# A three-stage decoder layer: a smaller move in memory, the last batch's router earlier, its last norm and store tile by tile

## The chip, the core and the metric

The kernel runs on one core of one Trainium2 chip. The metric is the device time of one execution in microseconds; lower is better. TensorE does the matrix products, VectorE (DVE), ScalarE (ACT) and GpSimd (POOL) the elementwise work, and SyncE (SP) issues all DMAs. Each engine works through its own instruction stream in order, and the engines wait for each other only at semaphores.

## The reference, cut to what matters

For 16 batches of 256 tokens with 512 channels, three sublayers follow each other, each added to its input and then normalised over the channels:

```
x = layernorm(x + attention(x) @ Wo + bo)      # 16 heads of 128, 4 KV heads, rotary, causal softmax
x = layernorm(x + wkv(w, u, k=x, v=context))   # running maximum and decayed sums over the tokens
x = layernorm(x + ffn(x))
# ffn(x):
h      = silu(x @ rw1.T + rb1)                 # 64 hidden channels
logits = h @ rw2.T + rb2 + gates               # 16 experts
coeff  = softmax over the top 2 of logits, zero elsewhere
out    = x @ W.T + bias + sum_e coeff[e] * (x @ A[e].T) @ B[e].T     # rank 16 each
```

## The kernel before

Every fp32 operand of a large product is split into a high and a low part, and a product is three matmuls (lines 527 to 529): high by high, high by low, low by high. TensorE does all of them in one stream.

The attention runs over 256 head positions (32 pairs of a half of the heads and a batch, 8 heads each). `run` walks through slots n; in each slot an engine does, for different heads at fixed lags, projection, scores, transposed probabilities, value product and output product. The weights come in as 40 raw pieces (`load_piece`), which ScalarE copies to the high part and DVE subtracts to the low part (`splits`, the subtraction is L1405). `SPLIT_AT` says in which slot ScalarE splits a piece; DVE does it one slot later (`behind=1`), at the end of its slot; SP issues the load up to three slots earlier. Ten staging areas in the WKV buffers hold raw pieces; the piece of head 4's query weights is the ninth and sits in the buffer `ED`.

In slot 3 DVE multiplies the third query head by the cosines (L1162, on ScalarE's bias at L772), then makes the low part of a V tile (L1192). TensorE's projections use two PSUM banks in turn, and so the projection of the fourth head waits for that V tile's low part (`proj_free`). The rotated half of a head pair is fetched by two DMAs, SW<-QB (L422, L423), POOL multiplies it by the sines (L1008), adds it (L1011) and makes the low part Ql (L1019), on which the scores (L596) wait.

The WKV recurrence of a batch ("tail") and the feed-forward stage ("step") are laid into the same slots at lags given by tables. A step k has three parts, and different batches stand at different stages in it: batch k-1 is turned, k-2 goes through router and low-rank products, k-3 through the dense product, k-4 through the last norm. Batches are counted in order of their feed-forward; the last is 15. So in step 17 TensorE does, in this order: low-rank products and router input of batch 15 (part 0), turn of batch 14's weighted low-rank rows (L700); dense(0) of batch 14, turn of batch 15's hidden tile (L712), in part 1; dense(1) of batch 14, logits of batch 15 (L721, four matmuls, on `hid_copied` from ScalarE), second low-rank product of batch 14, in part 2. In step 18 TensorE turns batch 15's weighted rows first (L700, on `weighted` from POOL), then does its dense products.

Between logits and `weighted` lie DVE's top 2 (L1382 to L1397) and POOL's coefficients (L1109 to L1113) and weighting (L1118). Behind the dense and low-rank products DVE adds the residual, a 128-token tile at a time (L1350, `out_sum`), the first tile in part 2 of step k and the second in part 0 of the next; then `norm_stats` (L1236, L1239, L1241) takes both tiles, POOL makes the inverse root and the shift (L1087 to L1091), ScalarE scales both tiles (L942), and SP stores the batch with one DMA of 512 KB (L485).

Buffers are allocated in order of their `sb` calls: W (81920 bytes per partition) first, then smalls, tables, Bo, XR, X and the rest.

Of the kernel before, what the change touches and what calls it, by code (L numbers as in the profile page):

```python
# [18 lines left out]
EPS = 1e-5  # L19
# [10 lines left out]
for i in range(PAIRS):  # L30
    f = i % 2
# [9 lines left out]
def ro_buf(b):  # L41
# [23 lines left out]
NP = JL + 2 + 2 * HEADS  # L65

FIRST_ORDER = [PK, PK + 1, PQ, PQ + 1, PV, PV + 1] + list(range(PQ + 2, NP))
SPLIT_AT = [[-6, -6, -2, -2, -6, -6, 0, 1, 1, 2, 3, 4] + [h // 2 + 4 for h in range(HEADS)],
            [7, 8, 10, 11] + [h + 11 for h in range(HEADS)] + [h + 19 for h in range(HEADS)]]
RELOAD_AT = [-10, -9, -6, -5] + [h - 6 for h in range(HEADS)] + [h + 3 for h in range(HEADS)]  # L70
KEEP_AT = [2, 3, 4, 5] + [h + 4 for h in range(HEADS)] + [h + 9 for h in range(HEADS)]
# [7 lines left out]
TAIL_BATCH = [b for i in range(PAIRS) for b in (2 * i + 1, 2 * i)]  # L79
# [95 lines left out]
def decoder(nc, xt, xn, ctxt, wraw, small, bo, wf, wl, wb, fbias, trig_t, late_t, out):  # L175
    fp32, fr, u32 = mybir.dt.float32, mybir.dt.float32r, mybir.dt.uint32
    ALU, ACT = mybir.AluOpType, mybir.ActivationFunctionType

    ctx = ExitStack()
    with ctx:  # L180
        def sb(name, shape, dt=fp32):
            return ctx.enter_context(nc.sbuf_tensor(name, shape, dt))
# [12 lines left out]
        wq_tile = lambda i, h, kc: W[:, PQ + h, i, kc * HD:(kc + 1) * HD]  # L195
        wo_tile = lambda i, h: W[:, PO + h, i, :]

        smalls = sb("smalls", [P, 160])
        cols = lambda at, n: smalls[:, at:at + n]
        by_half = lambda a: a.rearrange("p (f h) -> p f h", f=HALVES)  # L200
        Bk, Bq, Bv = by_half(cols(0, 4)), by_half(cols(4, 16)), by_half(cols(20, 4))
        Wb, Ub = cols(24, KC), cols(28, KC)
        Iota, Rb2, Gates, Rb1, Rw2 = cols(32, 16), cols(48, 16), cols(64, 16), cols(80, HID), smalls[0:HID, 144:160]

        late = sb("tables", [P, TT * C + P])
        tables = late[:, 0:TT * C]
        Cos, Sin, Mask = tables[:, 0:T], tables[:, T:2 * T], tables[:, TT * C - P - T:TT * C]
        Ident = late[:, TT * C:TT * C + P]
        Bo = sb("Bo", [P, C])

        XR = sb("XR", [P, KC, T])
# [75 lines left out]
        HST = SW[0:HID, 0, :]  # L287
        HB, HE = (SW[:, 1, a * P:(a + 1) * P].rearrange("p (a k) -> p a k", a=TT) for a in range(2))
        LOW = sb("LOW", [P, TT, EXP * RANK])
        Fb = Bo  # L290
        per_row = lambda a, n: a.rearrange("p (a k) -> p a k", a=1).to_broadcast([P, TT, n])
        STF = sb("STF", [P, 2, TT, 6])
        MVF = sb("MVF", [P, 2, TT, 2])
        VEF = sb("VEF", [P, 2, TT])
        RSF = sb("RSF", [P, 2, TT])
        NMF = sb("NMF", [P, 2, TT])

        s_flat = S[:, :, :].rearrange("p a n -> p (a n)")
# [92 lines left out]
        def run(eng, slot, splits=None, ffn_weights=None, step=None, ahead=0, behind=0):  # L391
# [11 lines left out]
            for n in range(FIRST_STEP_BEHIND, STEPS):  # L403
                for part in range(3):
                    step(n, part)

        def stage_of(n, lag):
            return n - lag if 0 <= n - lag < BATCH else None

# [3 lines left out]
        def _(sp):  # L413
# [55 lines left out]
            def step(n, part):  # L469
                f = stage_of(n, 0)  # L470
                if f is not None and part == 0:
                    b = TAIL_BATCH[f]
                    if f >= 2:
                        sp.wait_ge(biased, f - 1)
                        sp.wait_ge(f_turned, TT * (f - 1))
                    elif f == 1:
                        sp.wait_ge(q_lo, ALL // 2)
                    else:
                        sp.wait_ge(x2_out[2], x2_stored(13))
                    sp.wait_ge(x2_out[ro_buf(b)], x2_stored(b))  # L480
                    sp.dma_start(XF[f % 2], mixed[b, :, :].rearrange("(a p) c -> p a c", p=P)).then_inc(f_in[f % 2], 16)
                f = stage_of(n, 4)
                if f is not None and part == 2:
                    sp.wait_ge(f_done, f + 1)
                    sp.dma_start(out[TAIL_BATCH[f], :, :].rearrange("(a p) c -> p a c", p=P), OUT[f % 2]).then_inc(f_out[f % 2], 16)  # L485

            def load_piece(u):
                if u >= STAGES:
# [30 lines left out]
            sp.dma_start(late[:, TT * C - P - T:TT * C + P], late_t).then_inc(const_in, 16)  # L519
            run(sp, slot, splits, ffn_weights, step, ahead=AHEAD)  # L520
            for i in range(2):
                sp.wait_ge(f_out[i], 16 * BATCH // 2)

        @block.tensor
        def _(pe):
# [128 lines left out]
            def step(n, part):  # L654
                def turn_x2(t):
                    f = stage_of(n, 1)
                    if f is not None:
# [8 lines left out]
                            last = nc.tensor.transpose(bank[t][:, c * P:(c + 1) * P], XF[f % 2][:, t, c * P:(c + 1) * P], Ident[:, :])  # L666
                        last.then_inc(f_turned, 1)

                def dense(t):
                    f = stage_of(n, 3)  # L670
                    if f is not None:
                        if f == 0 and t == 0:
                            pe.wait_ge(acc_read, READS[POS - 1] + 1)
                            pe.wait_ge(w_lo, HALVES * NP + 2 * KC)
                        above(pe, f_sum, TT * (f - 1) + t + 1)
                        for k in range(KC):
                            last = three(bank[5 + t][:, :], [x[:, f % 2, k, t * P:(t + 1) * P] for x in X],
                                         [wf_tile(i, k) for i in range(2)], k == 0, False)
                        last.then_inc(dense_done, 1)
# [22 lines left out]
                elif part == 1:  # L702
                    dense(0)
                    turn_x2(0)
                    f = stage_of(n, 2)
                    if f is not None:
                        pe.wait_ge(silu_done, f + 1)
                        if f == 0:
                            pe.wait_ge(ot_lo, ALL // 2)
                        above(pe, lg_b, f)  # L710
                        for t in range(TT):
                            last = nc.tensor.transpose(bank[4][0:HID, t * P:(t + 1) * P], HE[:, t, :], Ident[:, :])  # L712
                        last.then_inc(hid_turned, 1)
                else:
                    dense(1)
                    turn_x2(1)
                    f = stage_of(n, 2)
                    if f is not None:
                        pe.wait_ge(hid_copied, f + 1)
                        for a in range(TT):  # L720
                            last = nc.tensor.matmul(bank[4][:, T + a * EXP:T + (a + 1) * EXP], HST[:, a * P:(a + 1) * P], Rw2, start=True, stop=True)  # L721
                        last.then_inc(logits_done, 1)
                    f = stage_of(n, 3)
                    if f is not None:
                        pe.wait_ge(wt_lo, f + 1)
# [11 lines left out]
        def _(act):  # L737
# [161 lines left out]
            def step(n, part):  # L899
# [26 lines left out]
                elif part == 1:  # L926
# [10 lines left out]
                        copy(HST, bank[4][0:HID, 0:T]).then_inc(hid_copied, 1)  # L937
                    f = stage_of(n, 4)
                    if f is not None:
                        act.wait_ge(f_shift, f + 1)  # L940
                        for t in range(TT):
                            last = nc.scalar.activation(OUT[f % 2][:, t, :], OUT[f % 2][:, t, :], ACT.Identity,  # L942
                                                        bias=NMF[:, f % 2, t:t + 1], scale=RSF[:, f % 2, t:t + 1])
                        last.then_inc(f_done, 1)
                else:
                    x_hi_tile(1)
                    f = stage_of(n, 2)
# [27 lines left out]
        def _(pool):  # L975
# [106 lines left out]
            def step(n, part):  # L1082
                f = stage_of(n, 4)
                if f is not None and part == 0:
                    pool.wait_ge(f_ve, f + 1)
                    above(pool, f_done, f - 1)
                    gp.tensor_tensor(RSF[:, f % 2, :], VEF[:, f % 2, :], Mhalf[:, :], ALU.pow).then_inc(f_rs, 1)  # L1087
                    pool.wait_ge(f_rs, f + 1)
                    gp.tensor_tensor(NMF[:, f % 2, :], MVF[:, f % 2, :, 0], RSF[:, f % 2, :], ALU.mult).then_inc(f_rs2, 1)
                    pool.wait_ge(f_rs2, f + 1)  # L1090
                    gp.tensor_scalar(NMF[:, f % 2, :], NMF[:, f % 2, :], -1.0, None, ALU.mult).then_inc(f_shift, 1)  # L1091
                f = stage_of(n, 2)
                if f is not None and part == 1:
                    pool.wait_ge(f_in[f % 2], 16 * (f // 2 + 1))
# [31 lines left out]
        def _(dve):  # L1126
# [104 lines left out]
                probabilities(n)  # L1231
                tail(n, 0)

            def norm_stats(tiles, par, stats, mv, ve, done):
                for t in range(TT):
                    v.bn_stats(stats[:, par, t, :], tiles[:, t, :])  # L1236
                dve.drain()
                for t in range(TT):
                    v.bn_aggr(mv[:, par, t, :], stats[:, par, t, :])  # L1239
                dve.drain()  # L1240
                v.tensor_scalar(ve[:, par, :], mv[:, par, :, 1], EPS, None, ALU.add).then_inc(done, 1)  # L1241

            def norm_shift(par, mv, rs, nm):
                v.scalar_tensor_tensor(out=nm[:, par, :], in0=mv[:, par, :, 0], scalar=-1.0, in1=rs[:, par, :],
# [90 lines left out]
            def step(n, part):  # L1335
# [16 lines left out]
                if part == 0:  # L1352
                    out_sum(4, 1)
                    f = stage_of(n, 4)
                    if f is not None:
                        dve.wait_ge(f_sum, TT * f + TT)
                        above(dve, f_shift, f - 1)
                        norm_stats(OUT[f % 2], f % 2, STF, MVF, VEF, f_ve)
                    f = stage_of(n, 2)
                    if f is not None:  # L1360
                        dve.wait_ge(hid_read, TT * f + TT)
# [13 lines left out]
                else:  # L1375
                    x_lo_tile(1)
                    f = stage_of(n, 2)
                    if f is not None:
# [19 lines left out]
                        dve.wait_ge(top_p2, f + 1)  # L1398
                        dve.wait_ge(lg_sum, f + 1)
                    out_sum(3, 0)  # L1400

            def splits(hf, i):
                u = nth_piece(hf, i)
# [72 lines left out]
```

## Time and profile before

| | |
|---|---|
| median of 3 runs | 1619.72 us (1618.47 to 1620.61) |
| the profiled execution | 1619.31 us |
| its span, first to last instruction | 1617.5 us |
| TensorE matmuls busy | 1554.8 us, 96% |
| DVE, ACT, POOL busy | 83%, 69%, 63% |
| granted TensorE clock, mean | 0.989 of full |

Busy shares are means over the whole span. TensorE is full nearly everywhere but at the two ends, so the views that count are the timelines and the chain of waits there. All positions are microseconds from the span's start.

### The profile page before, as it was taken

The numbers are of one execution on the slowest core, as the hardware profiler recorded it, in microseconds if no ns is written. First come the engines' busy times: TensorE is split into PE (matmuls) and PEld (weight loads), VectorE is DVE, ScalarE is ACT, GpSimd is POOL, SyncE is SP. The second block draws the span as 40 slices with busy tenths as digits, with TensorE's granted clock in tenths as the row PEclk, the third lists the DMA queues.
The fourth block names the chain that finished last, engine by engine and source line by source line (L and its number), as shares of the span: only waits on it lengthen the run. The fifth ranks groups of instructions, "written<-read, shape, count | busy, mean of one in ns | idle before, by whom it ended". The sixth has DMA issues, their size and how long they took to land.

```text
span 1617.5 us, 32631 instructions
## 1 busy us (share of the span) xinstructions
PE 1554.8 (96%) x10464; PEld 1411.9 (87%) x10464; DVE 1341.2 (83%) x3431; ACT 1117.2 (69%) x2995; POOL 1013.3 (63%) x852
## 2 busy tenths in 40 slices
PE   7999999999999999999999999999999977989997
PEld 7899999999999999999999999999999866777885
DVE  6776698889888988898989898888988885867864
ACT  6877787877787778777877787878777764334332
POOL 3665586758675767576767676767676642735653
PEclk9999999999999999999999999999999998999999
DMA  8766344324442444244424442444244412121211
GB/s 291 249 215 217 112 141 147 112 73 152 143 131 65 146 149 136 55 149 147 137 59 151 151 137 60 151 151 137 60 147 153 142 51 86 53 87 70 79 66 52
DMA packets 81624, 202.61 MB, mean 125 GB/s; under 512 B 10416, under 2 KB 11056, under 8 KB 81456
## 3 DMA queue, kind: packets, MB, share of 16 engines
q1 hardware_dynamic: 81456, 200.53, 39.4%
q8 instruction: 85, 1.39, 0.3%
q14 instruction: 83, 0.68, 0.1%
HBM read 120.80 MB, written 37.75 MB: 98 GB/s over the span
## 4 chain that ended last, share of the span: by engine, by line
PE 80%; DVE 8%; issue 3%; POOL 3%; ACT 2%; DMA 1%; DVEq 1%; SPq 0%; ACTq 0%; POOLq 0%
PE bank L527 24%; PE bank L528 23%; PE bank L529 23%; PE bank L651 5%; PE bank L596 2%; PE bank L642 1%; PE bank L634 1%; PE bank L597 1%; DMA SW<-QB 1%; DVE PS L1302 1%; DVE QS L1295 1%; PE bank L666 1%; DVE ED L1313 1%; DVEq L1383 1%; DVE RC L1162 0%
## 5 line engine op out<-in xcount | busy, mean ns | idle before, releaser
L527 PE MATMUL bank<-Xh,W 128*128 128x256 f32 x1280 | 363.6, 284 | 10.8 <-DVE W L1405 7.2
L528 PE MATMUL bank<-Xl,W 128*128 128x256 f32 x1280 | 362.1, 283 | 0.0
L529 PE MATMUL bank<-Xh,W 128*128 128x256 f32 x1280 | 361.8, 283 | 0.0
L1019 POOL TENSOR_TENSOR Ql<-RC,Qh 128x512 fp32r<-128x512 f32 x128 | 170.1, 1329 | 213.0 <-ACT Qh L739 213.0
L754 ACT ACTIVATE S<-S,NM 128x128 f32<-128x128 f32 (+1 forms) x512 | 228.1, 447 | 66.4 <-DVE NM L1147 65.9
L527 PEld LDWEIGHTS bank<-Xh,W 128*128 128x128 f32 x1280 | 242.9, 190 | 13.6 <-DVE Xl L1208 7.2
L739 ACT ACTIVATE PTh<-bank 128x384 fp32r<-128x384 f32 x256 | 125.1, 489 | 173.6 <-PE bank L651 173.6
L1008 POOL TENSOR_TENSOR SW<-SW,tables 128x512 f32<-128x512 f32 x128 | 170.2, 1330 | 116.8 <-DMA SW<-QB 116.7
L528 PEld LDWEIGHTS bank<-Xl,W 128*128 128x128 f32 x1280 | 243.4, 190 | 0.0
L529 PEld LDWEIGHTS bank<-Xh,W 128*128 128x128 f32 x1280 | 243.3, 190 | 0.0
L739 ACT ACTIVATE S<-S,RL 128x128 f32<-128x128 f32 (+1 forms) x512 | 203.5, 447 | 31.5 <-DVE RL L1154 31.4
L527 PE MATMUL bank<-W,OTh 128*128 128x512 f32 x512 | 203.6, 398 | 10.8 <-DVE OTl L1217 7.1
L528 PE MATMUL bank<-W,OTh 128*128 128x512 f32 x512 | 203.8, 398 | 0.0
L529 PE MATMUL bank<-W,OTl 128*128 128x512 f32 x512 | 203.2, 397 | 0.0
L1011 POOL TENSOR_TENSOR RC<-RC,SW 128x512 f32<-128x512 f32 x128 | 180.4, 1409 | 18.9 <-POOL SW L1008 0.9
L527 PE MATMUL bank<-W,Xh 128*128 128x256 f32 (+2 forms) x512 | 167.1, 326 | 1.7 <-DVE RC L1162 1.4
L528 PE MATMUL bank<-W,Xh 128*128 128x256 f32 (+2 forms) x512 | 163.4, 319 | 0.0
L529 PE MATMUL bank<-W,Xl 128*128 128x256 f32 (+2 forms) x512 | 163.3, 319 | 0.0
L1162 DVE SCALAR_TENSOR_TENSOR RC<-bank,smalls,tables 128x256 f32<-128x256 f32 x256 | 119.5, 467 | 42.5 <-ACT QB L772 42.4
L1133 DVE TENSOR_TENSOR PTl<-bank,PTh 128x384 fp32r<-128x384 f32 x256 | 141.1, 551 | 2.9 <-ACT PTh L739 2.3
L1143 DVE TENSOR_TENSOR S<-bank,tables 128x128 f32<-128x128 f32 x256 | 72.5, 283 | 78.0 <-PE bank L529 77.6
L651 PE MATMUL bank<-tables,S 128*128 128x128 f32 x768 | 126.2, 273 | 1.0 <-DVE PTl L1133 1.0
(155 smaller groups left out, 4446.6 us busy)
## 6 DMA issues: line engine op xcount, KB each, us to landing
W<-kept SPq DMA_DIRECT2D x140, 512.0 KB, 4.4
SW<-QB SPq DMA_DIRECT2D x256, 128.0 KB, 2.3
kept<-W SPq DMA_DIRECT2D x40, 512.0 KB, 4.7
XR<-XR SPq DMA_DIRECT2D x64, 128.0 KB, 2.3
RO<-in_xn SPq DMA_DIRECT2D x16, 512.0 KB, 4.0
KVT<-in_ctxt SPq DMA_DIRECT2D x16, 512.0 KB, 4.3
mixed<-RO SPq DMA_DIRECT2D x16, 512.0 KB, 4.0
XR<-in_xt SPq DMA_DIRECT2D x15, 512.0 KB, 5.1
```

Of the source, the lines that this page charges most:

```text
L527: nc.tensor.matmul(dst, lhs[0], rhs[0], start=first, stop=False)
L528: nc.tensor.matmul(dst, lhs[0], rhs[1], start=False, stop=False)
L529: return nc.tensor.matmul(dst, lhs[1], rhs[0], start=False, stop=last)
L651: last = nc.tensor.transpose(pt_ps[:, k * P:(k + 1) * P], S[:, g % 2, k * P:(k + 1) * P], Ident[:, :])
L739: return nc.scalar.activation(dst, src, ACT.Copy, **kw)
L754: last = nc.scalar.activation(S[:, i, c], S[:, i, c], ACT.Exp, bias=NM[:, i, t:t + 1], scale=-1.0, accum_out=L[:, i, t:t + 1])
L1008: gp.tensor_tensor(SW[:, :, :], SW[:, :, :], both(Sin), ALU.mult).then_inc(q_sin, 1)
L1011: gp.tensor_tensor(RC[:, i % 2, :, :], RC[:, i % 2, :, :], SW[:, :, :], ALU.add).then_inc(q_summed, 1)
L1019: gp.tensor_tensor(Q[1][:, :, :], RC[:, i % 2, :, :], Q[0][:, :, :], ALU.subtract).then_inc(q_lo, 1)
L1133: v.tensor_tensor(PT[1][:, g % 4, :], pt_ps[:, 0:P + T], PT[0][:, g % 4, :], ALU.subtract).then_inc(pt_lo, 1)
L1143: v.tensor_tensor(S[:, i, 0:P], s_ps[:, P:T], Mask[:, 0:P], ALU.add).then_inc(masked, 1)
L1162: v.scalar_tensor_tensor(out=RC[:, g // 2 % 2, g % 2, :], in0=proj_ps("Q", g, 0), scalar=Bq[:, SEQ[g // HEADS][0], h:h + 1], in1=Cos[:, :] ...
```

## The change

There are four edits. The small table `smalls` (640 bytes per partition) is allocated behind `LOW`, and the four statistics buffers of the last norm (96, 32, 16 and 16 bytes) ahead of `Bo`. The split of head 4's query weights goes from slot 1 to slot 2. In step 17 the logits of batch 15 come right behind its L712 in part 1, instead of behind dense(1). And for batch 15 alone, the last norm and the store go tile by tile: DVE takes tile 0's statistics behind its sum in part 2 of step 18, POOL and ScalarE do a tile at a time, and SP issues two stores of 256 KB.

```
-SPLIT_AT = [[-6, -6, -2, -2, -6, -6, 0, 1, 1, 2, 3, 4] + [h // 2 + 4 for h in range(HEADS)],
+SPLIT_AT = [[-6, -6, -2, -2, -6, -6, 0, 1, 2, 2, 3, 4] + [h // 2 + 4 for h in range(HEADS)],
...
-        smalls = sb("smalls", [P, 160])          # now behind LOW
...
+        STF = sb("STF", [P, 2, TT, 6])           # were behind LOW; MVF, VEF, RSF too
...
@@ SP, part 2 of a step, stage 4
+                        for t in range(TT):
+                            sp.wait_ge(f_done, f + t + 1)
+                            sp.dma_start(rows[:, t, :], OUT[f % 2][:, t, :]).then_inc(f_out[f % 2], 16)
...
@@ TensorE, part 1 of a step, behind the turn of the hidden tile
                         last.then_inc(hid_turned, 1)
+                        if f == LAST:
+                            logits()
                 else:
                     dense(1)
                     turn_x2(1)
-                    f = stage_of(n, 2)
-                    if f is not None:
-                        pe.wait_ge(hid_copied, f + 1)
-                        for a in range(TT):
-                            last = nc.tensor.matmul(bank[4][:, T + a * EXP:T + (a + 1) * EXP], HST[:, a * P:(a + 1) * P], Rw2, start=True, stop=True)
-                        last.then_inc(logits_done, 1)
+                    if stage_of(n, 2) != LAST:
+                        logits()
...
@@ ScalarE
-                        act.wait_ge(f_shift, f + 1)
                         for t in range(TT):
+                            act.wait_ge(f_shift, f + 1 + t * (f == LAST))
...
-                        last.then_inc(f_done, 1)
+                            if f == LAST or t == TT - 1:
+                                last.then_inc(f_done, 1)
...
@@ GpSimd
+                    for k, those in enumerate((slice(0, 1), slice(1, 2)) if f == LAST else (slice(0, TT),)):
+                        pool.wait_ge(f_ve, f + k + 1)
...
@@ DVE, norm_stats over a range of tiles; part 0, then part 2
-                        norm_stats(OUT[f % 2], f % 2, STF, MVF, VEF, f_ve)
+                        norm_stats(OUT[f % 2], f % 2, STF, MVF, VEF, f_ve, range(f == LAST, TT))
...
                     out_sum(3, 0)
+                    if stage_of(n, 3) == LAST:
+                        dve.wait_ge(f_sum, TT * LAST + 1)
+                        dve.wait_ge(f_shift, LAST - 1)
+                        norm_stats(OUT[LAST % 2], LAST % 2, STF, MVF, VEF, f_ve, range(1))
```

## Rows read from the trace of the kernel before

**Rows 1.** Windows, mid-kernel: busy of PE, PEld, DVE, ACT, POOL, clock, DMA share, GB/s
```profile
200.00:400.00 200.00, 199.65 (x1408) 183.80 (x1407) 179.35 (x453) 154.85 (x423) 140.20 (x101) 1.00 0.40 123
```

**Rows 2.** Chain of waits around the last logits: start us, us, what
```profile
1587.57 0.44 PE bank L700 x4
...
1590.81 0.22 PE bank L712 x2
...
1593.80 0.56 PE bank L721 x4
...
1598.46 1.21 POOL QB L1118 x2
...
1599.71 0.66 PE bank L700 x4
```

**Rows 3.** Timelines of ACT and PE, same stretch: start, duration, what, idle before it
```profile
1591.06 0.38 ACT L739 ACTIVATE SW<-bank 64x256 f32<-64x256 f32 x1 [1.53 <-PE bank L712]
...
1596.93 0.40 PE L529 MATMUL bank<-W,Ql 128*128 128x512 f32 x1
```

**Rows 4.** Chain of waits behind the last matmul
```profile
1608.78 0.70 DVE XR L1350
...
1611.18 0.18 DVE VEF L1241
...
1612.77 0.81 ACT XR L942
1613.58 0.71 ACTq L180
```

**Rows 5.** Timelines of DVE and SP behind the last matmul
```profile
1607.38 0.69 DVE L1350 TENSOR_TENSOR XR<-bank,KRC 128x512 f32<-128x512 f32 x1 [5.65 <-PE bank L529]
...
1609.50 1.28 DVE L1236 BATCH_NORM_STATS2 STF<-XR 128x6 f32<-128x512 f32 x2
...
1614.32 0.37 SPq L485 DMA_DIRECT2D out_x<-XR  x1
```

**Rows 6.** DMA view, 1600 to 1618: GB/s in 40 slices; an issue's KB and landing
```profile
GB/s 0 0 0 0 0 0 0 0 182 423 396 164 0 0 0 0 0 0 0 0 0 0 0 0 0 0 0 0 0 0 0 0 0 73 405 419 269 0 0 0
...
out_x<-XR SPq DMA_DIRECT2D x1, 512.0 KB, 2.7
```

**Rows 7.** Timelines of DVE, ACT, POOL and PE around the first long idle time
```profile
19.15 1.75 DVE L1405 TENSOR_TENSOR W<-ED,W 128x512 fp32r<-128x512 f32 x1
20.83 0.47 DVE L1162 SCALAR_TENSOR_TENSOR RC<-bank,smalls,tables 128x256 f32<-128x256 f32 x1
21.22 0.41 DVE L1192 TENSOR_TENSOR Vl<-bank,Vh 128x256 fp32r<-128x256 f32 x1
...
19.69 0.47 ACT L772 ACTIVATE QB<-bank,smalls 128x256 f32<-128x256 f32 x1 [1.41 <-PE bank L529]
...
19.05 1.31 POOL L1008 TENSOR_TENSOR SW<-SW,tables 128x512 f32<-128x512 f32 x1 [0.37 <-DMA SW<-QB]
...
21.78 0.40 PE L527 MATMUL bank<-Xh,W 128*128 128x256 f32 x1 [2.13 <-DVE Vl L1192]
```

**Rows 8.** Chain of waits through the start
```profile
34.10 4.94 DMA SW<-QB
...
55.38 0.39 PE bank L596
```

**Rows 9.** Windows of PE in the start, first and last of four: busy, clock, DMA share
```profile
24.00:26.00 2.00, 2.00 (x14) 0.66 0.87 334
...
30.00:32.00 2.00, 2.00 (x18) 1.00 0.85 306
```

**Rows 10.** Timeline of PE in mid-kernel
```profile
708.26 0.28 PE L529 MATMUL bank<-PTh,Vl 128*128 128x256 f32 x1
708.38 0.28 PE L527 MATMUL bank<-Xh,W 128*128 128x256 f32 x1
708.50 0.28 PE L528 MATMUL bank<-Xl,W 128*128 128x256 f32 x1
```

More of the change, by code:

```diff
@@ L196, in decoder @@
         wo_tile = lambda i, h: W[:, PO + h, i, :]
-        smalls = sb("smalls", [P, 160])
[L199 to L203, printed above, removed]
         late = sb("tables", [P, TT * C + P])
@@ L208, in decoder @@
         Ident = late[:, TT * C:TT * C + P]
+        STF = sb("STF", [P, 2, TT, 6])
+        MVF = sb("MVF", [P, 2, TT, 2])
+        VEF = sb("VEF", [P, 2, TT])
+        RSF = sb("RSF", [P, 2, TT])
         Bo = sb("Bo", [P, C])
@@ L289, in decoder @@
         LOW = sb("LOW", [P, TT, EXP * RANK])
+        smalls = sb("smalls", [P, 160])
+        cols = lambda at, n: smalls[:, at:at + n]
+        by_half = lambda a: a.rearrange("p (f h) -> p f h", f=HALVES)
+        Bk, Bq, Bv = by_half(cols(0, 4)), by_half(cols(4, 16)), by_half(cols(20, 4))
+        Wb, Ub = cols(24, KC), cols(28, KC)
+        Iota, Rb2, Gates, Rb1, Rw2 = cols(32, 16), cols(48, 16), cols(64, 16), cols(80, HID), smalls[0:HID, 144:160]
         Fb = Bo
         per_row = lambda a, n: a.rearrange("p (a k) -> p a k", a=1).to_broadcast([P, TT, n])
[L292 to L295, printed above, removed]
         NMF = sb("NMF", [P, 2, TT])
@@ L405, in run @@
                     step(n, part)
+        LAST = BATCH - 1
         def stage_of(n, lag):
@@ L483, in step @@
                 if f is not None and part == 2:
-                    sp.wait_ge(f_done, f + 1)
-                    sp.dma_start(out[TAIL_BATCH[f], :, :].rearrange("(a p) c -> p a c", p=P), OUT[f % 2]).then_inc(f_out[f % 2], 16)
+                    rows = out[TAIL_BATCH[f], :, :].rearrange("(a p) c -> p a c", p=P)
+                    if f < LAST:
+                        sp.wait_ge(f_done, f + 1)
+                        sp.dma_start(rows, OUT[f % 2]).then_inc(f_out[f % 2], 16)
+                    else:
+                        for t in range(TT):
+                            sp.wait_ge(f_done, f + t + 1)
+                            sp.dma_start(rows[:, t, :], OUT[f % 2][:, t, :]).then_inc(f_out[f % 2], 16)
             def load_piece(u):
@@ L521, in _ @@
             for i in range(2):
-                sp.wait_ge(f_out[i], 16 * BATCH // 2)
+                sp.wait_ge(f_out[i], 16 * (BATCH // 2 + (i == LAST % 2)))
         @block.tensor
@@ L667, in turn_x2, with logits @@
                         last.then_inc(f_turned, 1)
+                def logits():
+                    f = stage_of(n, 2)
+                    if f is not None:
+                        pe.wait_ge(hid_copied, f + 1)
+                        for a in range(TT):
+                            last = nc.tensor.matmul(bank[4][:, T + a * EXP:T + (a + 1) * EXP], HST[:, a * P:(a + 1) * P], Rw2, start=True, stop=True)
+                        last.then_inc(logits_done, 1)
                 def dense(t):
@@ L1084, in step @@
                 if f is not None and part == 0:
-                    pool.wait_ge(f_ve, f + 1)
                     above(pool, f_done, f - 1)
[L1087 to L1091, printed above, removed]
+                    for k, those in enumerate((slice(0, 1), slice(1, 2)) if f == LAST else (slice(0, TT),)):
+                        pool.wait_ge(f_ve, f + k + 1)
+                        gp.tensor_tensor(RSF[:, f % 2, those], VEF[:, f % 2, those], Mhalf[:, those], ALU.pow).then_inc(f_rs, 1)
+                        pool.wait_ge(f_rs, f + k + 1)
+                        gp.tensor_tensor(NMF[:, f % 2, those], MVF[:, f % 2, those, 0], RSF[:, f % 2, those], ALU.mult).then_inc(f_rs2, 1)
+                        pool.wait_ge(f_rs2, f + k + 1)
+                        gp.tensor_scalar(NMF[:, f % 2, those], NMF[:, f % 2, those], -1.0, None, ALU.mult).then_inc(f_shift, 1)
                 f = stage_of(n, 2)
@@ L1232, in odd, with norm_stats @@
                 tail(n, 0)
-            def norm_stats(tiles, par, stats, mv, ve, done):
-                for t in range(TT):
+            def norm_stats(tiles, par, stats, mv, ve, done, which=range(TT)):
+                for t in which:
                     v.bn_stats(stats[:, par, t, :], tiles[:, t, :])
                 dve.drain()
-                for t in range(TT):
+                for t in which:
                     v.bn_aggr(mv[:, par, t, :], stats[:, par, t, :])
                 dve.drain()
-                v.tensor_scalar(ve[:, par, :], mv[:, par, :, 1], EPS, None, ALU.add).then_inc(done, 1)
+                those = slice(which.start, which.stop)
+                v.tensor_scalar(ve[:, par, those], mv[:, par, those, 1], EPS, None, ALU.add).then_inc(done, 1)
             def norm_shift(par, mv, rs, nm):
```

## The prediction

> **What bounds the kernel now.** I read the windows by stage first. In 200 to 400 us TensorE is busy 199.65 of 200 us at full clock and no other engine comes near it [rows 1]. The stages from 60 us to about 1300 us look the same, so only the two ends can give time back. I read the end next, in the chain of waits. TensorE finishes the last turn of the hidden tile (L712) at 1591.03, does the second dense half of batch 14, and only then does the logits of batch 15 (L721) at 1593.80. From them hangs a serial chain: top-2 on DVE, coefficients and the weighting on POOL (L1118, ends 1599.67), and TensorE takes up again at 1599.71 [rows 2]. Its last matmul of batch 14 ended at 1597.33 [rows 3], so 2.38 us are idle. Behind the last matmul comes a second serial chain, in which the two tiles go together through sum, statistics, root, scaling and store [rows 4, 5]. The start came last, in the timelines of each engine: TensorE stands 2.13 us before 21.78, and its releaser is the last of a row of DVE instructions [rows 7].
>
> **Part 1, logits earlier.** In the step that holds the last batch's router, the four L721 matmuls go behind L712 and ahead of dense(1). They read HST, which ScalarE copies at 1591.06 for 0.38 us [rows 3], so TensorE now waits on that copy. The copy ends at 1591.44. The logits start at about 1591.50 and take 0.56 us [rows 2]. Queued behind this new wait are dense(1) and the low-rank products of batch 14, 24 matmuls. They start at 1592.06 instead of 1591.03, but the 0.56 us of logits is gone from between them, so the net delay is 0.47 us. After a wait the four L700 took 0.66 us against 0.44 us without one [rows 2]; if the logits pay the same 0.22 us, the delay is 0.69 us. So TensorE ends batch 14 between 1597.80 and 1598.02.
>
> The other arm: logits done at 1594.36 led to the weighting done at 1599.67, 5.31 us later. From 1592.06 to 1592.28 the same 5.31 us give 1597.37 to 1597.59. DVE and POOL have nothing else pending then; on ScalarE the scaling of batch 13 follows the copy and ends before the exponent is wanted. TensorE is therefore the later arm, by some 0.4 us, and of the chain's 2.3 us only the idle 2.38 less the delay 0.47 to 0.69 comes back: 1.69 to 1.91. The L700 group then no longer follows a wait: 0.44 instead of 0.66 [rows 2], 0.22 more. Sum 1.91 to 2.13 us; I take 2.05. Everything behind it (the two dense halves of batch 15 are 24 matmuls, 5.5 us at the 2.77 us that twelve took between L712 and L721 [rows 2], and in them DVE and ScalarE split the turned low-rank rows, two instructions of 0.7 us at most) moves up by as much. Bounds: 1.4 if both arms meet badly, 2.4 if no wait is left at all.
>
> **Part 2, last norm by halves.** I write times as before, unshifted. The sum of tile 0 starts at 1607.38 and takes 0.69 [rows 5]; today DVE then waits to 1608.78 for tile 1 [rows 4]. Now tile 0's statistics fit in: from the first statistics to the end of L1241 took 1609.50 to 1611.36, 1.86 us for two tiles, of which 1.28 are the two L1236 [rows 4, 5]. One tile less is 0.60 plus some 0.08 of L1239, so 1.18. Tile 0 is through at 1609.27, which makes tile 1's sum 0.5 us late; it ends 1609.98, its statistics 1611.18. That is only 0.18 before the old 1611.36: the half that DVE saves behind it is mostly paid ahead of it. POOL needs 1.41 from there to the scaling (1611.36 to 1612.77), the same for one column. Its first round (to 1610.7) is over before the second begins at 1611.2. ScalarE then scales one tile, not two: it saves the second, 0.71 [rows 4]. Store of tile 0 is issued at 1611.5, out of the way. The last store is 256 KB instead of 512 KB. Its traffic today is 2.7 us from issue to landing, and 405 to 419 GB/s while it moves [rows 6]; 256 KB less at 400 GB/s is 0.65. A store's fixed part may hide some of that: bounds 0.2 and 0.8. The extra issue (0.37 [rows 5]) is for tile 0 and lies beside the work on tile 1. Sum 0.18 + 0.71 + 0.65 = 1.54, bounds 0.9 and 1.8. The ends together give 3.6 us.
>
> **Part 3, one weight piece a slot later.** The subtraction W<-ED at 19.15 (1.75 us, ends 20.90) stands on DVE ahead of the cosine product (L1162, 20.83) and the V remainder (L1192, 21.22), and TensorE waits for that remainder. ScalarE's bias, which the cosine product needs, ended at 20.16 [rows 7]. Without the subtraction it starts at 20.19, and TensorE goes on at 21.13 instead of 21.78: 0.65. The piece then is subtracted behind K's remainder in the next slot, still 2 us before TensorE asks for it, and its 0.63 on ScalarE lies in an idle time. How much of the 0.65 survives is the question. The chain runs later through a swap's DMA that lands 4.94 us after issue [rows 8], behind a full queue. The queue can only give back time that it leaves unused: in four windows of 2 us from 24 to 32 its share was 0.87, 0.82, 0.93 and 0.85, 1.06 us unused in sum [rows 9]. Bounds: +2.3 (0.65, and the half-clock stretch after the idle time, mean clock 0.66 in 24 to 26 [rows 9], goes too, as the idle time is shorter) and -0.9 (two more POOL steps of the next chain cross a DVE subtraction; the one here took 1.75). I take 0.4, the nearer to the queue's rows.
> The rows show what such a crossing costs: the subtraction started 0.10 us after POOL's product (19.05, 1.31 us) and ended 0.54 after it [rows 7]. By the Trainium skill, SBUF — State Buffer, "Who interferes with whom", a DVE instruction with two SBUF inputs and a GpSimd one that reads SBUF exclude each other for the whole instruction, and the second waits. The trace agrees. It speaks against the change: the moved subtraction now meets POOL's Ql, on which the first scores wait; that would cost up to 0.7 there, against 1.9 us of slack.
>
> **Part 4, addresses.** The small table of 640 bytes goes behind, four statistics buffers (160 bytes, each rounded up to 32: 192) go ahead: the moves are 448 for x and all behind, 640 for the tables. I cost it at nothing. The matmul pitch at 256 columns is 0.12 us whether the moving operand is PT or X [rows 10], and these start at 224 and 128 bytes past a multiple of 256; both move to 32 and 192. The bounds are one nanosecond either way on each matmul with X or K moving (by the code 256 heads by 17 and 64 K tiles by 12, 5120), 5.1 us; no row supports either, and the far side is rival D.
> By the Trainium skill, DMA: Bandwidth & Descriptors, "How a descriptor splits into AXI transactions", a read that doesn't start at a multiple of 256 B fetches unused bytes. By it QB's swap reads get 64 bytes worse of some 2,200 and the rows' stores 192 better; both are hidden, and the sum stays.
>
> **Sum.** 2.05 + 1.54 + 0.4 = 4.0 us. The profiled execution took 1619.31 (span 1617.5 and 1.8 around it), 0.4 below the median of 1619.72, well inside the 2.1 us between the runs. From the profiled one the sum gives 1615.3, from the median 1615.7. I say 1615.6.
>
> **Rivals.**
> A, the forecast: 1614.7 to 1616.9, chance 0.56.
> B, the start gives its upper bound, because the half-clock stretch behind 22 us goes: 1.9 more, 1613.8. For it: TensorE would stand 1.48 us, not 2.13 [rows 7]. Against: the full queue of DMAs behind [rows 8]. Chance 0.15.
> C, a gain is lost: the store's fixed part stays (-0.45), the start gives nothing (-0.4) or loses 0.9, or the logits pay a full weight load: 1616.9 to 1618.5. Chance 0.21.
> D, slower than before: a moving operand that starts on an odd multiple of 64 bytes (X now does) is read more slowly. Place: the 5120 matmuls of part 4, all on the path that sets the end; it decides from 0.8 ns each (4.0 us), at 1 ns gives 1620.8 and at 1.5 ns 1623.4. Against it stands the equal pitch of PT, which isn't even on a multiple of 64. Chance 0.08, half of it beyond the bound.
>
> **How the numbers follow.** About 0.2%, 3.2 us, is what a measurement can tell from no change; faster means below 1616.5. Of A six sevenths lie there (0.48), all of B (0.15) and a little of C (0.02): 0.65. Same: the rest of A, of C and half of D: 0.31. Slower: 0.04. The range leaves out D and the outer parts of B and C: 1613.4 to 1618.2.
>
> **What would show it.** L721 right behind L712 with some 0.5 us idle on TensorE between; no idle time before the last L700; the span from last matmul to end about 1.5 shorter (8.8 before); two stores of tile halves, the last landing in about 2.1; TensorE going on at 21.1, and the last wait at the start, now at 55.38 [rows 8], at 55.0. Wrong would be: a different pitch in mid-kernel, L700 still waiting on POOL, or the last wait at the start later than 55.4.

## The result, and the profile after

The changed kernel takes 1606.64 us (median of 5 runs, 1604.41 to 1609.12), the one before 1620.61 (5 runs, 1618.47 to 1624.56). The ratio is 0.991, with an interval from 0.9893 to 0.9927: 14 us less, where 4.0 were forecast. The time lies outside the range of 1613.4 to 1618.2.

I cut both profiled executions at the same four events of TensorE: the last matmul of the Q projection of heads 16 and 255, the last four low-rank transposes (L700 before, L717 after), and the last matmul.

| stage | before, us | after, us | difference | forecast |
|---|---|---|---|---|
| start to head 16 | 88.25 | 85.63 | -2.6 | -0.4 |
| head 16 to head 255 | 1215.68 | 1208.34 | -7.3 | 0 |
| head 255 to the last four transposes | 295.78 | 292.84 | -2.9 | -2.05 |
| from there to the last matmul | 8.63 | 8.46 | -0.2 | 0 |
| last matmul to the end | 9.18 | 7.35 | -1.8 | -1.54 |

The last matmul counts from its start. Half of the gain is in the middle, where no instruction was changed. The lines of the changed kernel are numbered 9 higher for the three matmul lines (L536 to L538), 15 to 22 higher further down.

The middle, windows of the changed kernel (columns as in [rows 1]):
```profile
200.00:400.00 200.00, 199.16 (x1412) 183.17 (x1411) 179.12 (x452) 156.24 (x428) 144.41 (x105) 1.00 0.41 127
```
TensorE is as full as in [rows 1], and does 1412 matmuls instead of 1408. Over 1100 us it shows plainly. Kernel before, then changed kernel, TensorE alone (busy, matmuls, clock, DMA share, GB/s):
```profile
100.00:1200.00 1100.00, 1098.55 (x7753) 1.00 0.41 127
```
```profile
100.00:1200.00 1100.00, 1096.27 (x7794) 1.00 0.42 128
```
The same stream, 41 matmuls further, at the same full clock and with slightly more idle time: each matmul comes sooner behind the one before it.

The last logits, chain of waits, and the timelines of TensorE, ScalarE and POOL there; they answer to [rows 2, 3]:
```profile
1579.87 0.23 PE bank L729 x2
...
1580.56 0.61 PE bank L683 x4
...
1586.97 0.44 PE bank L717 x4
```
```profile
1580.56 0.61 PE L683 MATMUL bank<-smalls,SW 64*128 64x16 f32 x4 [0.47 <-ACT SW L754]
...
1580.13 0.38 ACT L754 ACTIVATE SW<-bank 64x256 f32<-64x256 f32 x1 [1.48 <-PE bank L729]
...
1585.28 1.20 POOL L1135 TENSOR_TENSOR QB<-LOW,S 128x256 f32<-128x256 f32 x2
```
The logits wait 0.47 us for the copy. POOL ends the weighting at 1586.48, TensorE comes to the transposes only at 1586.81, and the four take 0.44 us, as without a wait.

Behind the last matmul, timelines of DVE, POOL, ScalarE and SP, then the DMA view; they answer to [rows 4 to 6]:
```profile
1594.33 0.69 DVE L1368 TENSOR_TENSOR XR<-bank,KRC 128x512 f32<-128x512 f32 x1 [4.15 <-PE bank L538]
1595.05 0.69 DVE L1253 BATCH_NORM_STATS2 STF<-XR 128x6 f32<-128x512 f32 x1
...
1596.15 0.68 DVE L1368 TENSOR_TENSOR XR<-bank,S 128x512 f32<-128x512 f32 x1
...
1597.89 0.15 DVE L1259 TENSOR_SCALAR VEF<-MVF 128x1 f32<-128x1 f32 x1
...
1598.13 0.58 POOL L1104 TENSOR_TENSOR RSF<-VEF,Mhalf 128x1 f32<-128x1 f32 x1 [0.58 <-DVE VEF L1259]
...
1597.58 0.81 ACT L957 ACTIVATE XR<-XR,NMF,RSF 128x512 f32<-128x512 f32 x1 [4.96 <-POOL NMF L1108]
1599.32 0.81 ACT L957 ACTIVATE XR<-XR,NMF,RSF 128x512 f32<-128x512 f32 x1 [0.93 <-POOL NMF L1108]
...
1598.42 2.08 SPq L494 DMA_DIRECT2D out_x<-XR  x2
```
```profile
out_x<-XR SPq DMA_DIRECT2D x2, 256.0 KB, 2.0
```
Two tiles go through one behind the other, and a store of half the size lands 2.0 us after its issue, not 2.7.

The start, timelines of DVE, POOL and TensorE, which answer to [rows 7], and two windows of TensorE there, which answer to [rows 9]:
```profile
17.58 1.45 DVE L1427 TENSOR_TENSOR W<-E2Z,W 128x512 fp32r<-128x512 f32 x1
19.97 0.48 DVE L1179 SCALAR_TENSOR_TENSOR RC<-bank,smalls,tables 128x256 f32<-128x256 f32 x1 [0.94 <-ACT QB L787]
20.37 0.42 DVE L1209 TENSOR_TENSOR Vl<-bank,Vh 128x256 fp32r<-128x256 f32 x1
...
22.41 2.37 DVE L1427 TENSOR_TENSOR W<-ED,W 128x512 fp32r<-128x512 f32 x2
...
22.45 1.78 POOL L1035 TENSOR_TENSOR Ql<-RC,Qh 128x512 fp32r<-128x512 f32 x1 [0.74 <-ACT Qh L754]
...
20.93 0.36 PE L536 MATMUL bank<-Xh,W 128*128 128x256 f32 x1 [1.51 <-DVE Vl L1209]
...
24.29 0.39 PE L605 MATMUL bank<-KHL,Qh 128*128 128x256 f32 x1 [0.29 <-POOL Ql L1035]
```
```profile
22.00:26.00 4.00, 3.52 (x28) 1.00 1.00 375
36.00:40.00 4.00, 4.00 (x26) 0.68 1.01 314
```
The subtraction is gone from between, TensorE goes on at 20.93, and the stretch at half clock behind 22 us did not come. One came later: the mean granted clock from 36 to 40 us is 0.68, between the two levels of 2.4 and 1.2 GHz. The kernel before has one there too (0.58 from 22 to 26 us, 0.62 from 36 to 40).

### The profile page after: what moved, and what is told of

It reads as the page before. It is cut to its first block, busy times and chain, and to the rows that moved or that the text cites. A ratio compares the mean times of both kernels' runs of the same rounds, so it can differ in the third digit from the quotient of the medians.

```text
span 1602.6 us, 32639 instructions
## 1 busy us (share of the span) xinstructions
PE 1542.2 (96%) x10464; PEld 1400.7 (87%) x10464; DVE 1328.5 (83%) x3432; ACT 1117.1 (70%) x2995; POOL 1014.6 (63%) x855
## 4 chain that ended last, share of the span: by engine, by line
PE 79%; DVE 10%; issue 4%; POOL 3%; ACT 2%; DVEq 1%; DMA 1%; SPq 0%; POOLq 0%; ACTq 0%
PE bank L536 24%; PE bank L537 23%; PE bank L538 23%; PE bank L660 5%; PE bank L605 2%; DVE PS L1320 1%; PE bank L643 1%; PE bank L606 1%; PE bank L651 1%; DVE QS L1313 1%; DVE ED L1331 1%; DVE RC L1179 1%; ACT Xh L754 1%; PE bank L675 1%; DVE OTl L1234 1%
## 5 line engine op out<-in xcount | busy, mean ns | idle before, releaser
L536 PE MATMUL bank<-Xh,W 128*128 128x256 f32 x1280 | 360.3, 281 | 12.1 <-DVE W L1427 7.2
L538 PE MATMUL bank<-Xh,W 128*128 128x256 f32 x1280 | 359.5, 281 | 0.0
L536 PEld LDWEIGHTS bank<-Xh,W 128*128 128x128 f32 x1280 | 242.8, 190 | 14.9 <-DVE Xl L1225 7.2
L538 PEld LDWEIGHTS bank<-Xh,W 128*128 128x128 f32 x1280 | 243.7, 190 | 0.0
L536 PE MATMUL bank<-W,OTh 128*128 128x512 f32 x512 | 203.1, 397 | 11.9 <-DVE OTl L1234 8.2
L538 PE MATMUL bank<-W,OTl 128*128 128x512 f32 x512 | 202.9, 396 | 0.0
L536 PE MATMUL bank<-W,Xh 128*128 128x256 f32 (+2 forms) x512 | 166.5, 325 | 1.7 <-DVE RC L1179 1.7
L538 PE MATMUL bank<-W,Xl 128*128 128x256 f32 (+2 forms) x512 | 162.6, 318 | 0.0
```

The lines of the kernel that those rows point to most:

```text
L536: nc.tensor.matmul(dst, lhs[0], rhs[0], start=first, stop=False)
L538: return nc.tensor.matmul(dst, lhs[1], rhs[0], start=False, stop=last)
```

## The experiments

All timed ratios are against the kernel before. "Stretch" is the time from head 16 to head 255 in the profiled execution. Pitch is the mean time between the starts of neighbouring matmuls inside a unit of twelve (Q projection of a head), read from the trace between 100 and 1290 us. The distance of two buffers is that of their start addresses in a partition.

**Each part alone.** Four kernels, each the kernel before with one edit.

layout_only, the order of the buffers:
```
-        smalls = sb("smalls", [P, 160])      # behind W -> behind LOW
+        STF, MVF, VEF, RSF                   # behind LOW -> ahead of Bo
```


> Only the buffers' order is changed (smalls behind LOW, the four statistics buffers ahead of Bo). Theory A (addresses): the changed kernel's mid-part, from the last Q projection of head 16 to that of head 255, is 7.3 us shorter because the matmul pitch with X moving fell from 119 to 117 ns, and this comes from the addresses; then this kernel keeps some 7 to 8 us of the 14, ratio 0.995, and the Q units show the mean pitch of 116 to 117 ns. Theory B (phase): the pitch follows from when the other engines work beside TensorE, set at the start by the weight piece a slot later; then this kernel is at 1620, ratio 1.000, pitch 118.7 ns.

split_only:
```
-SPLIT_AT = [[-6, -6, -2, -2, -6, -6, 0, 1, 1, 2, 3, 4] ...
+SPLIT_AT = [[-6, -6, -2, -2, -6, -6, 0, 1, 2, 2, 3, 4] ...
```


> Only the weight piece of head 4 is split a slot later. Theory A: 1 to 2.6 us less, all of it before 90 us, pitch in mid-kernel 118.7 ns as before; ratio 0.999. Theory B: some 10 us less (2.6 at the start and 7.3 in mid-kernel), ratio 0.994, pitch 116 to 117 ns.

logits_only:
```
                         last.then_inc(hid_turned, 1)
+                        if f == LAST:
+                            logits()
```


> Only the logits of the last batch go ahead of dense(1). Both theories: 2.0 us less, all between the last L712 and the last group of four weighted-row transposes, start and mid-kernel as before, ratio 0.9988. If it gives more than 3, something else hangs on the order of TensorE's stream.

norm_only (statistics, root, scaling and store of the last batch by tiles, the buffers at their old places):
```
+                        norm_stats(OUT[LAST % 2], LAST % 2, STF, MVF, VEF, f_ve, range(1))
...
+                            sp.dma_start(rows[:, t, :], OUT[f % 2][:, t, :]).then_inc(f_out[f % 2], 16)
```


> Only the last norm and store by tiles. Both theories: from the last matmul to the end 7.4 us instead of 9.2, 1.8 us less, the rest as before, ratio 0.9989.

| kernel | median us (runs) | ratio, interval | head 16 at | stretch | pitch ns |
|---|---|---|---|---|---|
| before | 1620.82 (29) | 1 | 88.25 | 1215.68 | 118.7 |
| layout_only | 1612.12 (6) | 0.9948, 0.9932 to 0.9963 | 87.76 | 1208.53 | 116.4 |
| split_only | 1619.53 (12) | 0.999, 0.9979 to 1.0 | 86.78 | 1214.64 | 118.6 |
| logits_only | 1618.32 (12) | 0.9994, 0.9983 to 1.0004 | 89.63 | 1215.40 | 118.7 |
| norm_only | 1616.78 (12) | 0.9975, 0.9963 to 0.9988 | 87.12 | 1215.77 | 118.6 |

layout_only, TensorE from 100 to 1200 us (7753 matmuls in the kernel before):
```profile
100.00:1200.00 1100.00, 1096.38 (x7798) 1.00 0.41 128
```
The addresses alone make the stretch 7.2 us shorter, and the other three leave it within 1.1. Theory B (phase) is refuted. The ratios give 8.4, 1.6, 1.0 and 4.0 us, 15 together. The interval of logits_only has 1 inside it and that of split_only ends at 1, so for these two the traces carry the reading. In the traces the logits alone bring head 255 to the last transposes from 295.78 to 293.58 (2.2 us), and the norm alone the last matmul to the end from 9.18 to 7.31 (1.9 us). That norm_only's ratio says 4.0 (interval 1.9 to 6.0) is not explained by its trace, whose span is 3.1 us shorter, 1.1 of them ahead of head 16, where this kernel has no edit; the interval's lower end fits. The changed kernel gained 2.9 us in the stage from head 255 to the last transposes, 0.7 more than logits_only; which edit gave that is open, as layout_only's trace has 1.3 us less there than the kernel before and layout_x_back's, with x at its old address, 2.2 more.

**Which address.** layout_x_back: the new order, with `sb("pad0", [P, 112])` (448 bytes) ahead of XR.


> The new order of the buffers, and 448 unused bytes ahead of XR: tables, Bo, smalls stand at their new addresses, XR and all behind it at their old ones. If the addresses of x and what is behind it make the gain, the Q units (12 matmuls, 11 gaps) go back to a mean pitch of 118.7 ns and the stretch from head 16 to head 255 to 1215.7 us. If the tables or the small buffers make it, pitch 116.3 ns and 1208.5 us stay.


layout_only_x: the same 448 bytes behind X, ahead of KHL.


> The new order of the buffers, and 448 unused bytes behind X: XR and X are moved, K, V, Q, probabilities and all else behind are at their old addresses. If the address of the moving operand X alone counts, Q units run at 116.3 ns. If what DVE, ACT and POOL touch beside TensorE counts (Q, S, RC, PT), 118.7 ns. A value between means both.


pad64_x: the old order, `sb("pad0", [P, 16])` ahead of XR.


> The old order, and 64 unused bytes ahead of XR: 64 forward instead of 448 back, the same place modulo 512. If an address counts by its place within 64, 128, 256 or 512 bytes, the Q units run at 116.3 ns and the stretch takes 1208.5 us; if by a coarser place or by the distance to the weights or tables, another value.


pad128_x: the same with 32 columns.


> The old order, and 128 unused bytes ahead of XR. If only the place within 128 bytes counts, pitch 118.7 ns and 1215.7 us as before; if the place within 256 or more, a third value.


pad64_w: the old order, `sb("pad1", [P, 16])` ahead of W.


> The old order, and 64 unused bytes ahead of W, so that every buffer stands 64 bytes further and all distances stay. Theory C or D (distances between buffers count): Q units at 118.7 ns, head 16 to head 255 in 1215.7 us, as before. Theory E (a buffer's own place within 128 bytes counts): Q units at 116 ns and 1208 us, as with 64 bytes ahead of x.

TensorE in the same window as above, in the order layout_x_back, layout_only_x, pad64_x, pad128_x, pad64_w:
```profile
100.00:1200.00 1100.00, 1098.78 (x7752) 1.00 0.41 127
```
```profile
100.00:1200.00 1100.00, 1093.79 (x7802) 1.00 0.41 128
```
```profile
100.00:1200.00 1100.00, 1095.14 (x7792) 1.00 0.41 128
```
```profile
100.00:1200.00 1100.00, 1099.58 (x7730) 1.00 0.41 127
```
```profile
100.00:1200.00 1100.00, 1098.85 (x7758) 1.00 0.42 127
```

| kernel | X from W, modulo 256 | stretch us | pitch ns |
|---|---|---|---|
| before, pad64_w | 128 | 1215.68, 1215.23 | 118.7, 118.7 |
| layout_x_back | 128 | 1215.96 | 118.5 |
| layout_only, pad64_x | 192 | 1208.53, 1210.91 | 116.4, 115.9 |
| layout_only_x | 192, K and the rest at their old places | 1207.28 | 115.5 |
| pad128_x | 0 | 1219.36 | 119.7 |

Each stretch is that of a single execution, but kernels in which x, X and all behind stand alike lie within 1.3 us, or 3.6 where only x's distance modulo 256 is the same. The whole times are single ones too and give no ratio: 1622.24, 1611.90, 1610.89 and 1622.52 us for the first four beside 1616.85 for the kernel before, and 1619.49 for pad64_w beside 1615.19. The tables and the small buffers don't matter. x and X do, and not by their own place: 64 bytes ahead of W move everything, and the stretch stays. It is the distance between buffers. What stands behind X counts a little too: in layout_only_x the Q units are below both expected values (115.5), and the V units (W moving, X stationary) went from 117.8 ns in layout_only to 113.8, though X and W stand as there. pad64_x missed its expected 1208.5 us by 2.4. Whether the distance that counts is the one to the weights or to what other engines touch was open.

**Matmuls alone.** micro computes nothing of the reference. It runs units of 12 matmuls whose stationary operand starts at s and whose moving one at m:
```
for j in range(12):
    nc.tensor.matmul(bank[n % 2][:, 0:256], A[:, s // 4 + (n % 4 * 4 + j % 4) * 128:...+ 128],
                     M[:, m // 4 + j // 3 * 256:...+ 256], start=j == 0, stop=j == 11)
```


> A kernel of its own, not the decoder: 3 phases of 16 segments of 60 matmuls (128x256, fp32r, each with a weight load of its own). In the segments the stationary operand starts at 0 or 64 bytes and the moving one at 0, 32, 64 ... 224 bytes past its buffer's start (both buffers at multiples of 256 from each other). Phase 1: TensorE alone. Phase 2: DVE, ACT and POOL work beside it on other buffers; phase 3: the same, their buffers 64 bytes further. Theory C (TensorE's own two reads, moving operand and next weights, meet): the pitch in phase 1 differs between segments by 3 to 7 ns of 117, is high where both starts are equal modulo 128 and low where they are 64 apart, for both stationary starts. Theory D (the other engines' accesses meet TensorE's): phase 1 flat at 107 to 113 ns in all segments, and phases 2 and 3 higher and different from each other. Theory E (the moving start's own place counts): phase 1 depends on the moving start and not on the stationary one.

Windows of 6.6 us inside six segments: s/m = 0/0, 0/192, 64/0, 64/64 with TensorE alone, then 0/0 and 0/192 with three engines beside it (columns as in [rows 1]):
```profile
27.20:33.80 6.60, 6.60 (x58) 6.60 (x57) 0.00 (x0) 0.00 (x0) 0.00 (x0) 1.00 0.00 0
69.80:76.40 6.60, 6.60 (x60) 6.60 (x60) 0.00 (x0) 0.00 (x0) 0.00 (x0) 1.00 0.01 2
83.80:90.40 6.60, 6.60 (x61) 6.60 (x60) 0.00 (x0) 0.00 (x0) 0.00 (x0) 1.00 0.01 2
97.80:104.40 6.60, 6.60 (x58) 6.60 (x56) 0.00 (x0) 0.00 (x0) 0.00 (x0) 1.00 0.01 2
140.40:147.00 6.60, 6.60 (x58) 6.60 (x57) 6.60 (x5) 6.60 (x13) 6.60 (x4) 1.00 0.01 2
183.10:189.70 6.60, 6.60 (x61) 6.60 (x60) 6.60 (x5) 6.60 (x14) 6.60 (x5) 1.00 0.00 0
```

| m - s modulo 256 | 0 | 32 | 64 | 96 | 128 | 160 | 192 | 224 |
|---|---|---|---|---|---|---|---|---|
| s = 0, alone, ns | 120.0 | 117.9 | 117.8 | 119.8 | 118.7 | 117.4 | 113.9 | 118.3 |
| s = 64, alone | 119.8 | 117.9 | 117.8 | 119.8 | 118.7 | 117.4 | 113.5 | 118.3 |
| s = 0, others at work | 119.9 | 117.9 | 117.8 | 119.8 | 118.7 | 117.4 | 113.9 | 118.3 |

Theory C is the one that holds: the pitch goes with the distance between TensorE's own two operands. D is refuted by the third row (and phase 3 agrees with it within 0.1 ns), E by the second. The expected pattern modulo 128 was wrong: it is modulo 256. The decoder's 118.7 ns at 128 and 119.7 at 0 are these values; its 116.4 at 192 is not the 113.9.

micro2 is the same, TensorE alone, with finer and farther starts and other units ahead.


> Again matmuls and weight loads alone, nothing beside them: the moving start 0 to 240 bytes past a multiple of 256 from the stationary one in steps of 16; 192 and 0 with 256 to 1792 added; units of 256 columns behind units of other distances or of 512 columns; and 512 columns at 0 to 224. If the distance counts modulo 256 alone (theory C as the first such kernel showed it): 113.9 ns at 192 and 120.0 at 0 with whatever multiple of 256 added, and the same behind every other unit. If what ran before counts too (theory C with a memory), the same distance gives different pitches behind different units. For 512 columns a difference of 0 to 8 ns of 233.


At 192 with 256 to 1792 added the pitch is 113.3 every time, and at 0 with 256 to 1024 added it is 120.0, once the first unit is past. In steps of 16 there is a second low place, 112, with 113.3. What ran before counts: at 192 it is 113.3 behind units at 0, 128 and 192, and 117.8 behind units at 64. At 64 it is 117.8, but 113.3 behind a unit of 512 columns at 192. And at 32 it is 116.7, where micro had 117.9. Its windows at 192 behind 0, and at 192 behind 64:
```profile
184.20:189.60 5.40, 5.40 (x50) 1.00 0.02 3
210.20:215.60 5.40, 5.40 (x49) 1.00 0.00 0
```
With 512 columns the pitch is 226.7 at distance 0, 228.7 at 64 and 233 to 235 at all other multiples of 32.

**Does it hold for the other products, and is there a better version?** after_k_old: the changed kernel, 448 bytes behind X.


> The changed kernel with 448 unused bytes behind X, so that x and X stand at their new addresses and K, V, Q, the probabilities and all behind at their old ones. By the single look at the same layout without the other edits (head 16 to head 255 in 1207.3 us against 1208.5), this gives 1 us less than the changed kernel: 1605.6, ratio to before 0.9905. If that look was chance, 1606.6 as the changed kernel, ratio 0.991.


after_ot0:
```
+        sb("pad0", [P, 56])
         OT = [sb(f"OT{i}", [P, 2, 2, T], fr) for i in "hl"]
```


> The changed kernel with 224 unused bytes ahead of OT, so that OT (stationary of the output product) starts at a multiple of 256 from W (moving, 512 columns), where it was 32 past. Distance theory: 226.7 ns instead of 233.3 by the matmuls alone; the decoder's 1536 such matmuls go from 232 to 227 ns, 8 us less: 1598.6, ratio 0.986. Rival (only x's address matters, by something else): pitch 232 ns, 1606.6.


after_aligned:
```
+        sb("pad0", [P, 16])
         V = [sb(f"V{i}", [P, 2, TT, JL * HD], fr) for i in "hl"]
...
+        sb("pad1", [P, 40])
         PT = [sb(f"PT{i}", [P, 4, P + T], fr) for i in "hl"]
```


> The changed kernel with 64 unused bytes ahead of V and 160 ahead of PT: V, Q, PT and OT start at multiples of 256 from W, X and K stay 192 past. Distance theory: output product 8 us less; value product (PT moving, V stationary, distance 0) 226.7 instead of 232, 384 matmuls, 2 us less; scores (K moving, Q stationary, distance 192) 113.3 instead of 118 to 120 ns, 768 matmuls, 4 to 5 us less; in all 14 us: 1592.6, ratio 0.982. With the memory eating half: 1599. Rival: 1606.6.

| kernel | median us (runs) | ratio, interval | stretch us |
|---|---|---|---|
| changed | 1606.64 (5) | 0.991, 0.9893 to 0.9927 | 1208.34 |
| after_k_old | 1605.35 (5) | 0.9898, 0.9882 to 0.9914 | 1206.77 |
| after_ot0 | 1601.86 (4) | 0.9888, 0.9865 to 0.9911 | 1206.13 |
| after_aligned | 1598.86 (4) | 0.9875, 0.9851 to 0.99 | 1201.24 |

after_aligned, TensorE in the same window as above:
```profile
100.00:1200.00 1100.00, 1092.56 (x7840) 1.00 0.42 129
```
224 unused bytes seem worth some microseconds: after_aligned has 87 matmuls more than the kernel before in that window, and the lowest ratio of all. Against the changed kernel its stretch is 7.1 us shorter; but the intervals of the two ratios still overlap at one end, and those of after_k_old and after_ot0 overlap the changed kernel's widely. The gain did not come where it was expected, so that after_aligned's time is near the 1599 expected "with the memory eating half" is luck. The output product's matmuls went from 232.2 to 230.6 ns (after_ot0) and 230.2, not to 226.7; the value product did not move (231.7, then 230.9 and 231.6 ns), and the score's plain 256-column matmuls went from 119.1 to 117.2 and from 118.1 to 117.8, not to 113.3. Instead Q went to 114.7 ns and K and V units to 113.3 and 113.5 (V in the median, 114.2 in the mean), although X and W stand as in the changed kernel.

What runs ahead of a projection decides how much of x's distance it gets, as with micro2's units. Two Q units of the changed kernel, first and last of twelve matmuls, the first unit right behind the scores and the second right behind the value product:
```profile
705.41 0.28 PE L536 MATMUL bank<-Xh,W 128*128 128x256 f32 x1
...
706.70 0.28 PE L538 MATMUL bank<-Xh,W 128*128 128x256 f32 x1
...
711.64 0.28 PE L536 MATMUL bank<-Xh,W 128*128 128x256 f32 x1
...
712.91 0.28 PE L538 MATMUL bank<-Xh,W 128*128 128x256 f32 x1
```
The mean over the 117 Q units behind scores is 117.4 ns, over the 118 behind a value product 115.2. In the kernel before the two are 119.1 and 118.2, and in after_aligned, where the operands of the scores stand 192 apart and not 0, 114.4 and 115.1. So the changed kernel's 116.4 is a mean of two places, and neither is the 113.9 of the matmuls alone.

## Why the prediction was right or wrong

**Part 4, addresses, failed, and with it the size of the whole.** The step that failed is "I cost it at nothing": the new addresses are worth 8.4 us by layout_only's ratio (interval 6.0 to 11.0), 7.2 of them between heads 16 and 255. The zero rested on the equal 0.12 us of PT and X in [rows 10]. Two things were wrong in that step. First the scale: the spacing of two rows with two decimals can't tell 118.7 from 116.4 ns, and the 3840 projection matmuls with X moving make 9 us of 2.3 ns. Read as a mean over a stretch, the pitch has the needed digit. Second the quantity: I compared the moving operand's own place, but pad64_w and the matmuls alone show that the distance to the stationary operand counts, and PT and X have different partners. The text's bound of a nanosecond either way (5.1 us) was then left out of the range, as no row supported it; no row excluded it either, and 5.1 would have been too small. Rival D had the right instructions and the wrong sign. Among its signs of being wrong the prediction had named a different pitch in mid-kernel, and that is what came. A page speaks against this: the Trainium skill, TensorE: Matmul & The Clock Gate, "Step-by-step: what each phase is for", says that loading the next weights takes nothing from the running matmul's reads, as each has a port of its own. Here the pitch of matmuls with weight loads of their own goes from 113.3 to 120.0 ns when nothing but the distance of the two is changed. Which part of TensorE's path makes that is not shown: no run had matmuls without weight loads.

The rule that the prediction cites beside part 4 (the Trainium skill, DMA: Bandwidth & Descriptors, "How a descriptor splits into AXI transactions") can't be told in these runs: the swap's reads land after 2.3 us in both kernels (median), and the stores from RO, which should have gained, after 4.3 us where it was 4.0. No run changed these addresses alone.

**Part 1, logits, right.** The wait is 0.47 us, TensorE is the later arm (POOL 0.33 us ahead of it; forecast some 0.4), the transposes take 0.44. Forecast 2.05 us; logits_only's trace gives 2.2, its ratio 1.0 (interval -0.6 to 2.8).

**Part 2, the last norm, right, mis-sized by 0.3.** From the first sum to the last L1259 it took 3.71 us in the changed kernel and 3.98 before, so 0.27 (forecast 0.18). ScalarE saves one tile of 0.71, the store lands 0.7 sooner (forecast 0.65). The missing 0.15 is POOL's root: 0.58 us for one column, where I had kept the 0.72 of two columns.

**Part 3, the weight piece, right in its place, too small in its size.** TensorE stood 1.51 us, not 2.13 (forecast 1.48). The moved subtractions crossed POOL's Ql, which took 1.78 instead of 1.55 us, and TensorE waited 0.29 us for it. The last wait of the start moved from 55.38 to 53.05, and to 53.88 in split_only (forecast 55.0). In the five kernels that have this edit head 16 is reached at 85.4 to 87.4 us (mean 86.3), in the nine that don't at 86.9 to 89.6 (mean 88.1): 1.8 us, where I took 0.4. Part of that is the addresses: four of the five have x at distance 192, but only three of the nine, and among these seven alone the means are 86.2 and 87.3, 1.1 us apart. split_only's ratio gives 1.6 us (interval 0 to 3.4). The rest goes with rival B's mechanism. In all five the mean clock from 22 to 26 us is 1.00; of the nine without the edit it was 0.57 to 0.70 in five, and 1.00 in four. Ahead of head 16 the clock was at its lower level for 3.4 us in each of the five; in the nine for 3.4 us in two, 6.8 in three and 10.2 in four. So the start is a draw, and the edit seems to weight it; fourteen single traces make that likely and don't show it. My argument from the full DMA queue held the gain down too much.

**The rest.** Forecast parts 2.05 and 1.54, with split_only's 1.6 instead of 0.4, make 5.2 us; 8.4 of layout_only make 13.6, and 14.0 were measured. So close a fit is in part luck, as layout_only's interval alone is 5 us wide. Open are the 2 us that norm_only's ratio has above its trace, and what exactly the memory in the pitch is.

## What to carry to other kernels

Where TensorE is full for a thousand microseconds, read the pitch of its matmuls as a mean to a tenth of a nanosecond: one nanosecond on each of the 3840 projection matmuls is 3.8 us here, and the spacing of two rows rounded to 10 ns hides it. Any edit that shifts a buffer, even an unused pad, can change it, so a changed allocation must be tried by itself before its time is put down to another edit. An allocation order is cheap to search: a few pads of 64 bytes, each with the matmul count of a fixed window.

## What the runs showed of the hardware

- Matmuls of 256 columns with a weight load each come every 113.3 to 120.0 ns at full clock, by the distance between moving and stationary start modulo 256 bytes: low at 112 and 192, high at 0, 80 and 96. Other engines at work beside them change it by at most 0.1 ns.
- The same with 512 columns: 226.7 ns at distance 0, 228.7 at 64, 233 to 235 at other multiples of 32. The best distance isn't the same for both widths.
- The pitch depends also on what ran before: 113.3 or 117.8 ns at the same distance of 192, for all four units that followed; in the changed kernel 115.2 ns behind a value product and 117.4 behind scores.
- POOL's power of -0.5 takes 0.58 us for one column and 0.72 for two.
- A store of 256 KB to HBM lands 2.0 us after issue, one of 512 KB 2.7.
